# One of GpSimd's own rows in the numbering stage of a graph kernel, and column numbers read from PSUM

## The reference, cut to what matters

```python
edge_index = jnp.stack([src, dst])
x = _layernorm(x + _L0_gnn_ref(x, L0_gnn_W, L0_gnn_b, src, dst), axis=-1)
x = _layernorm(x + _L1_gnn_ref(x, edge_index, edge_attr_32, ...), axis=-1)
x = _layernorm(x + _L2_gnn_ref(x, src, dst, L2_gnn_W, L2_gnn_b), axis=-1)
x = _layernorm(x + _L3_gnn_ref(x, L3_gnn_W, L3_gnn_att_src, L3_gnn_att_dst, L3_gnn_bias, edge_index), axis=-1)
```

## Time and profile before

| what | value |
|---|---|
| median of 3 runs | 3892.95 us |
| lowest and highest of these | 3881.23 and 3897.71 us |
| the profiled execution's own time | 3893.57 us |
| its span in the trace | 3891.8 us |
| mean granted TensorE clock over the span | 0.641 of full speed |

### The profile page before, as it was taken

The page is one execution under the profiler, slowest core; times in us unless marked ns, Lnnn a source line. Parts: engine busy times, 40 slices in busy tenths (PEclk is TensorE's granted clock), DMA queues, the critical chain, the costliest instruction groups (busy, mean ns, idle before and its releaser), DMA issues. The chain is left out here.

```text
span 3891.8 us, 43254 instructions
## 1 busy us (share of the span) xinstructions
PE 1921.5 (49%) x9253; PEld 1516.3 (39%) x9253; DVE 2656.7 (68%) x9976; ACT 2088.9 (54%) x4590; POOL 2715.1 (70%) x2767
## 2 busy tenths in 40 slices
PE   5466600578776887875666637888830000000000
PEld 2233300477675777763444426777830000000000
DVE  8899963577775656656888868898944444444444
ACT  8688810466763222223455446777755555555555
POOL 0377777777774777757777747777637777777776
PEclk9799955688886666665555556666655555555555
DMA  0111186355554666654666645555522222222221
GB/s 7 32 38 38 38 260 200 102 163 163 156 159 141 203 210 196 204 178 151 202 199 201 197 149 173 191 197 187 187 77 77 81 80 76 76 81 80 77 77 60
DMA packets 355728, 521.93 MB, mean 134 GB/s; under 512 B 213275, under 2 KB 224964, under 8 KB 355466
## 3 DMA queue, kind: packets, MB, share of 16 engines
q1 hardware_dynamic: 261082, 363.50, 27.5%
q0 software_dynamic: 94384, 155.67, 15.7%
HBM read 227.76 MB, written 291.22 MB: 133 GB/s over the span
## 5 line engine op out<-in xcount | busy, mean ns | idle before, releaser
L1952 PE MATMUL l_psR<-l_diag,l_ones 128*128 128x128 f32 x2 | 0.8, 502 | 1003.9 <-DVE l_diag L1810 1003.9
L565 POOL DMA_INDIRECT O<-x_pad,nidx x393 | 407.6, 1037 | 119.7 <-issue 119.7
L1118 POOL DMA_INDIRECT l1b_G<-t,src x392 | 395.5, 1009 | 128.8 <-issue 118.1
L1720 POOL DMA_INDIRECT l_G<-t,src x392 | 378.1, 965 | 151.9 <-issue 119.1
L1118 POOL DMA_INDIRECT l1a_G<-t,src x392 | 386.0, 985 | 136.0 <-issue 117.0
L1735 POOL DMA_INDIRECT out<-O,nidx x393 | 389.2, 990 | 128.2 <-issue 118.8
L1427 POOL DMA_INDIRECT l_G<-t,src x392 | 379.6, 968 | 132.8 <-issue 117.4
L813 POOL DMA_INDIRECT l_G<-xs,src x392 | 370.5, 945 | 126.1 <-issue 115.5
L1952 PEld LDWEIGHTS l_psR<-l_diag,l_ones 128*128 128x128 f32 x2 | 0.5, 312 | 1004.0 <-DVE l_diag L1810 1004.0
L174 ACT ACTIVATE O<-O,l_shift,l_rstd 128x96 f32<-128x96 f32 x786 | 292.5, 460 | 27.6 <-DVE l_shift L168 27.6
L1286 PEld LDWEIGHTS l1b_psE<-l1b_we,l1b_edge 32*128 32x128 f32 x784 | 174.2, 323 | 240.5 <-DMA l1b_edge<-edge_k 181.3
(11 more groups left out here) (309 smaller groups left out, 6421.1 us busy)
## 6 DMA issues: line engine op xcount, KB each, us to landing
h<-l_G SPq DMA_DIRECT2D x96, 392.0 KB, 2.5
t<-l1b_t_out SPq DMA_DIRECT2D x48, 768.0 KB, 3.6
h<-l_G SPq DMA_DIRECT2D x48, 768.0 KB, 3.5
xs<-en_y SPq DMA_DIRECT2D x49, 392.0 KB, 5.0
en_y<-x_pad SPq DMA_DIRECT2D x49, 384.0 KB, 4.5
t<-l_t_out SPq DMA_DIRECT2D x48, 392.0 KB, 4.5
l_H<-t SPq DMA_DIRECT2D x48, 392.0 KB, 3.0
t<-l_tr_out SPq DMA_DIRECT2D x48, 384.0 KB, 3.0
```

The lines of the kernel that those rows point to most:

```text
L565: pool.indirect_dma_start(k.O[:, at, :], None, x, bass.IndirectOffsetOnAxis(k.nidx[:, at:at + 1], 0))\
L1118: pool.indirect_dma_start(tile(c)[:, q, :], None, table, bass.IndirectOffsetOnAxis(k.src[:, at:at + 1], 0))\
L1720: pool.indirect_dma_start(tile(c)[:, q, :], None, t4, bass.IndirectOffsetOnAxis(k.src[:, at:at + 1], 0))\
```

## The change

The number of exact low rows goes from three to four. VectorE still makes three of them, GpSimd makes the fourth, and ScalarE makes four signs in place of five. TensorE runs four matmuls into each bank, and waits for GpSimd's row before the fourth. GpSimd's rows are guarded by the same `tallied` as the others; it begins when `split` has written `lo`. The 128 numbers that VectorE compares for the high rows are copied once to a PSUM bank (`psI`, 64 words of 32 bits a partition), and the comparison reads them there in place of SBUF.

```diff
-    EXACT = 3
+    EXACT = 4
...
-        psC, psU, psO = ps("psC"), ps("psU"), ps("psO")
+        psC, psU, psO, psI = ps("psC"), ps("psU"), ps("psO"), ps("psI")
+        iota_hi = psI[:, 0:64].bitcast(F16)
...
+            pool.wait_ge(lo_known, 1)
+            for c in range(NCH):
+                if c >= 2:
+                    pool.wait_ge(tallied, c - 1)
+                at = c * Q + EXACT - 1
+                pool.tensor_scalar(hot_lo[:, c % 2, EXACT - 1, :], k.iota_lo[:, :], lo[:, at:at + 1], None,
+                                   ALU.is_equal).then_inc(pool_hot, 1)
             pool.wait_ge(start_known, 1)
...
-            split(dve, g[:, :], hi[:, :], lo[:, :], t[:, :], ti[:, :])
+            split(dve, g[:, :], hi[:, :], lo[:, :], t[:, :], ti[:, :]).then_inc(lo_known, 1)
...
             dve.wait_ge(consts, 7)
+            dve.tensor_copy(psI[:, 0:64], k.iota_hi[:, :].bitcast(F32))
+            dve.drain()
...
-                for q in range(EXACT):
+                for q in range(EXACT - 1):
                     dve.tensor_scalar(hot_lo[:, c % 2, q, :], k.iota_lo[:, :],
                                       lo[:, c * Q + q:c * Q + q + 1], None, ALU.is_equal)
-                dve.tensor_tensor(hot_hi[:, c % 2, :, :], k.iota_hi[:, :].unsqueeze(1).to_broadcast([128, Q, 128]),
+                dve.tensor_tensor(hot_hi[:, c % 2, :, :], iota_hi.unsqueeze(1).to_broadcast([128, Q, 128]),
...
                 for q in range(EXACT):
+                    if q == EXACT - 1:
+                        pe.wait_ge(pool_hot, c + 1)
                     pe.matmul(psC[:, 0:K], hot_hi[:, c % 2, q, :], hot_lo[:, c % 2, q, :],
```

More of the change, by code:

```diff
@@ L293, in numbering @@
         hot_ready = sem("hot_ready")
+        lo_known = sem("lo_known")
+        pool_hot = sem("pool_hot")
         upto_ready = sem("upto_ready")
```

## The result

| | before | changed |
|---|---|---|
| median of 8 runs | 3894.44 us | 3909.61 us |
| lowest to highest | 3880.18 to 3901.60 us | 3894.53 to 3912.88 us |
| profiled execution's own time | 3893.57 us | 3912.04 us |
| scan of psC starts | 139.64 us | 148.41 us |

The ratio is 1.0042 with a 95% interval of [1.0022, 1.0062]: 15 us slower, within the 0.5% that I called no change, but clear of the scatter and six times the 2.5 us that I forecast. The scan of the numbering stage, for which I had forecast 142 us, comes 8.8 us later than before. That leaves about 6 us of the 15 that are lost behind the stage. In time the interval of the ratio reaches from 9 to 24 us, so by the runs alone these 6 us may be anything from none to 15.

What follows compares the result with a forecast made beforehand. ScalarE's signs bound the numbering stage, VectorE next. Split and copy -12.8, GpSimd's hold-up of VectorE +14.7, start +0.6 make +2.5 us on 3893.6: 3896.1 us, about 3896 in the median; range 3878 to 3910 us.

Steps and rivals of the forecast that it cites:

- the chance of no change: Whole kernel: chance of 0.82 that the time stays within 0.5%, 19.5 us, of the kernel before.
- the sum's -12.8: Numbering stage: gain from four signs once VectorE comes last, before GpSimd's cost to VectorE: 12.8 us.
- 13.1 us less the copy: Numbering stage: scan 13.1 us earlier with VectorE last, less 0.3 us for copying the numbers to PSUM.
- C: High rows: numbers in PSUM make them faster, 1.13 to 0.7 us, gaining 25.1 us: 3868 us; chance 0.07.
- what GpSimd does to VectorE: Low rows and compress steps: GpSimd's 0.60 us row holds VectorE up, 1.5 us per round of five chunks.
- 14.7 + 0.6 us: Numbering stage: VectorE's hold-up by GpSimd over 9.8 rounds, 14.7 us, plus 0.6 us at the start.
- The bounds that I drew: GpSimd's row: 0.41 us at least, 0.77 us at most, with 0.60 us taken.
- Rival B: Low rows: GpSimd's row is long and VectorE waits behind it; at 1.5 us a row, 3927 us; chance 0.10.
- point of decision: GpSimd's row: the length, 1.11 us, from which the kernel would be 19.5 us slower.
- two buffers are enough to keep it going: VectorE and TensorE: a buffer is freed 1.6 us after `hot_hi`, VectorE needs it only 1.83 us later.
- the double buffer's reserve of 0.24 us: Numbering stage: GpSimd, released with the buffer, is 0.24 us ahead of VectorE's low rows.

Runs made afterwards that it cites:

- e1: Trial stage run ahead of the changed kernel's, without GpSimd's rows (eighth row set once): scan 16 us earlier than the changed kernel's, 127.8 us without VectorE's waits.
- e3: Changed kernel with fourteen extra matmuls keeping TensorE busy in each compress step: scan starts at 140.58 us, one run 3907.13 us.
- d1: Kernel before with fourteen additions on VectorE delaying the stage's end: scan at 148.93 us, median 5215.08 us, ratio 1.0002 on a slower chip.
- r2: Changed kernel measured again, unaltered, against the kernel before on a slower chip: scan at 147.54 us, median 5235.06 us, ratio 1.0043.
- x1: Kernel before with one unread GpSimd comparison of 128 x 128 numbers at the numbering stage's start: ratio 1.0041, scan at 139.86 us.
- x2: Kernel before with one unread GpSimd addition of two tensors at the numbering stage's start: last layer's scatters at a median of 982 to 986 ns.
- v3: Changed kernel with compress spread over four chunks and five ScalarE signs in two chunks of five: 5238.01 us, ratio 0.9981, noisy chip.
- v1: Kernel before, GpSimd silent, compress spread over four chunks, four exact rows in two chunks of five: 5265.35 us, ratio 1.0033, noisy chip.
- v4: Kernel before, GpSimd silent, compress spread over four chunks, four exact rows in two chunks of five: 5199.23 us, ratio 0.9981, steadier slow chip.
- e7: Changed kernel with each compress step's four instructions spread behind four successive chunks: scan 15.8 us earlier, at 132.6 us; one run 5263.81 us.
- e5: Changed kernel with the high rows' 128 numbers read from SBUF again, GpSimd's rows kept: scan at 148.58 us, one run 5290.72 us.

## Why the prediction was wrong

The measured 3909.6 us lies at the upper end of the range that I gave, 3910, and the chance of no change was given for what came, but the kernel did get slower by more than its scatter where I had forecast 2.5 us.

**Right: what the split gives (the sum's -12.8).** I had 13.1 us less the copy, a scan at 126.8; e1 without its waits gives 127.8. VectorE is the next limit, as forecast, and C did not come: the high rows are at 1.21 us.

**Right in sum by luck, wrong in its parts: what GpSimd does to VectorE.** Forecast 14.7 + 0.6 us, measured 12.8. But the row is 1.30 us and not 0.60, and the hold-up is 0.26 us of it and not 0.36 in every second chunk. Two errors cancelled. The bounds that I drew, 0.41 to 0.77 us, came from iota and select instructions, and the true row lies outside them: they were not the nearest in kind after all, as no row showed an instruction that takes one number per partition. Rival B had the length right (over its point of decision, 1.11 us) and the cost wrong: by its formula a row of 1.3 us holds VectorE up for 38.7 us, and the kernel would have been over 19.5 us slower. The Trainium skill, "SBUF — State Buffer", Who interferes with whom, says that the second of the two to come waits for the whole of the first; the trace does not agree. The measured L407 decides: its longest is 0.651 us, a third of a microsecond over a free one, beside GpSimd rows of 1.26 us and more.

**Wrong: "two buffers are enough to keep it going".** This is the step of the stage that failed: the sum has no term for VectorE's waits for TensorE, and the runs show 7.8 us of them. I took TensorE's 1.6 us from the end of `hot_hi` to the free buffer at the clock of the earlier trace rows. After a compress step TensorE has been idle for 3 us, its eight matmuls go at half speed, and the double buffer's reserve of 0.24 us is gone: VectorE waits after each of the nine compress steps, 1.07 us in the one shown and 8.2 us in all, and with the clock kept up the scan comes 7.8 us earlier (e3). Before, ScalarE's slower pace hid this: VectorE was ahead of it and the compress step fell into its slack, so that TensorE was fed every 2.56 us and its clock stood at 0.97. I had even read 0.91 in the earlier trace rows and gone past it. The stage's balance is then -11.8 (the split) + 12.8 (GpSimd) + 7.8 (clock) = +8.8 us. It closes by itself, as the three are differences between the same scans (139.64, 127.8, 140.58 and 148.41 us). What supports the parts are the counts beside it: 13.5 us more in the low rows, and 8.2 us of waits for TensorE.

**Not seen at all: the loss behind the stage.** The prediction let the stage's shift be the whole. The runs show some 6 us more on the first chip (15.2 - 8.8), of which 393 x 12 ns = 4.7 us are the scatters' own durations, and 20 us on the chip of d1 and r2. That the scatters get longer because GpSimd runs an arithmetic instruction at all is shown by x1 and x2. That this is also what costs the 20 us is not shown: the scatters account for 5 us of it in the profiles of that chip, and on the noisy chip v3 and v1 come out the other way round. So the loss of whole time on the slower chips stays open, and so does why the scatters and not the gathers pay.

**A version that beats both** is there only within limits. v4 takes 5199.23 us against 5208.76 of the kernel before on its chip, 0.9981 with an interval that ends at 1.0001, and 36 us less than the changed kernel; its stage is 8.2 us shorter in both of its profiles. The same kernel as v1, on the noisy chip, does not confirm it (1.0033, 0.9993 to 1.0073). Against before it stays unclear.

## What to carry to other kernels

When the engine that sets the pace is relieved, ask what the next one does in its longest step, and not only what it does on average: here a pause of 3 us that fed TensorE nothing cost again when it came back at 1.2 GHz, and spreading the pause over several chunks was worth more (15.8 us of stage) than the split itself gives (11.8 us). A row handed to GpSimd is not free for VectorE: it cost 0.26 us of VectorE's time where making the row costs 0.233, and some 0.1 us once the rhythm let it fall beside the high rows (e7). And measure a first use of GpSimd arithmetic by itself, with one useless instruction, before the real work goes there.

## What the runs showed that I had not expected

- One arithmetic instruction on GpSimd in the first stage makes the scatters from SBUF, thousands of us later, some 10 ns longer each (972 or 974 to 982 to 986 ns), while the medians of the gathers stay at 944 to 949.
- A comparison of 128 x 392 half-width numbers with one number per partition takes GpSimd 1.26 us at least, against 0.45 us for an iota of that size; of 128 x 128 full-width numbers 0.609 us (x1), and an addition of two such tensors 0.452 us (x2).
- Beside it, VectorE's fast low row is 0.3 us longer at most, and its two-tensor instruction of 1.21 us makes GpSimd's row longer when both its tensors lie in SBUF: a median of 1.74 us in place of 1.30 (e5).
- TensorE's granted clock was 0.86 from 20 to 120 us where VectorE's compress steps left it waiting for 3.07 us, and 1.00 where the same work left no wait over 1.1 us (e7).
